# First diffusion step: VectorE checks a pair first and then copies the mixed sums of its first tile

## The reference

```python
def _top_p_attention(X, W1, W2, W3):
    q = X @ W1.T @ W2.T
    k = X @ W3.T
    probs = jax.nn.softmax(q @ k.T / TAU, axis=-1)
    idx = jnp.argsort(-probs, axis=-1)
    sp = jnp.take_along_axis(probs, idx, axis=-1)
    cs = jnp.cumsum(sp, axis=-1)
    keep_sorted = cs - sp < TOP_P          # TOP_P = 0.9
    ...
    A = probs * mask
    return A / jnp.maximum(A.sum(-1, keepdims=True), 1e-12)
R = S + jnp.eye(N); R = R / R.sum(-1, keepdims=True)
for n in range(STEPS):                     # STEPS = 2
    A = _top_p_attention(Xa, W1, W2, W3)
    Xf = R @ Xf
    Xa = A @ Xa
    Z = Z + Xf @ U1[n].T + Xa @ U2[n].T
```

## Time and profile before

| | |
|---|---|
| median of three runs | 2990.27 us |
| the profiled execution's own time | 2988.41 us |
| its span, first to last instruction | 2986.7 us |
| mean granted TensorE clock | 0.895 of full speed |
| the first diffusion step, about | 900 to 1449 us of the span |

### The profile page before, as it was taken

One profiled execution on the slowest core, in us unless ns is written; L12 is line 12 of the kernel. 1 busy time (PEld: TensorE's weight loads), 2 busy tenths in 40 slices (PEclk: granted clock), 3 DMA queues, 4 the chain that ended last, 5 costly groups with the idle time before them and its releaser, 6 DMA issues. The chain is left out here.

```text
span 2986.7 us, 44231 instructions
## 1 busy us (share of the span) xinstructions
PE 2314.8 (78%) x14310; PEld 1703.0 (57%) x14310; DVE 1941.0 (65%) x4668; ACT 1224.8 (41%) x1981; POOL 662.2 (22%) x1649
## 2 busy tenths in 40 slices
PE   3499999589536999996844974877563599999999
PEld 2377777377315787775523763766462244444468
DVE  5567777523337877777238888888965577777741
ACT  3455566211346666661256863766422100000000
POOL 2000000200224444340025643555402200000000
PEclk9699999899768999998966987989787799999999
DMA  1322221054100000000100000000004000000013
GB/s 46 119 98 97 97 81 68 5 191 145 42 17 13 19 23 19 22 27 14 48 17 6 16 11 11 16 11 16 11 11 155 2 1 0 0 0 0 0 50 96
DMA packets 49299, 120.85 MB, mean 40 GB/s; under 512 B 5952, under 2 KB 24672, under 8 KB 45792
## 3 DMA queue, kind: packets, MB, share of 16 engines
q1 hardware_dynamic: 49120, 118.83, 11.8%
HBM read 93.85 MB, written 24.97 MB: 40 GB/s over the span
## 5 line engine op out<-in xcount | busy, mean ns | idle before, releaser
L1923 DVE SCALAR_TENSOR_TENSOR fil_acc<-bank,fil_node,fil_acc 128x256 f32<-128x256 f32 x682 | 330.0, 484 | 110.4 <-PE bank L1991 97.8
L1346 PE MATMUL bank<-idf,X 128*128 128x128 f32 x968 | 136.2, 302 | 202.9 <-DVE step_recips L1841 202.9
L1436 ACT ACTIVATE step_PT<-bank 128x512 f32<-128x512 f32 (+1 forms) x264 | 127.5, 577 | 357.4 <-PE bank L1346 357.4
L1989 PE MATMUL bank<-parts_in,fil_xTh 128*128 128x512 f16 x704 | 268.5, 381 | 0.0
L1991 PE MATMUL bank<-parts_in,fil_xTl 128*128 128x512 f16 x704 | 268.3, 381 | 0.0
L1990 PE MATMUL bank<-parts_in,fil_xTh 128*128 128x512 f16 x704 | 268.2, 381 | 0.0
L1346 PEld LDWEIGHTS bank<-idf,X 128*128 128x128 f32 x968 | 119.4, 154 | 215.4 <-DVE step_recips L1841 206.2
L722 PE MATMUL bank<-V,HL 128*128 128x256 f32 x968 | 236.4, 386 | 0.2
L1356 PE MATMUL bank<-kH,qHL 128*128 128x512 f16 (+1 forms) x264 | 105.9, 401 | 151.9 <-ACT step_E L1445 117.7
L1378 PE MATMUL bank<-A,step_PT 128*128 128x256 f32 x968 | 216.1, 379 | 0.0
L1378 PE MATMUL bank<-H,step_PT 128*128 128x256 f32 x968 | 216.0, 379 | 0.0
(11 more groups left out here) (382 smaller groups left out, 5044.4 us busy)
## 6 DMA issues: line engine op xcount, KB each, us to landing
gat_A<-in_adj SPq DMA_DIRECT2D x22, 1408.0 KB, 5.9
step_a<-adjT SPq DMA_DIRECT2D x44, 352.0 KB, 3.0
gcn_raw<-in_L_W SPq DMA_DIRECT2D x16, 512.0 KB, 4.7
split<-gcn_halves SPq DMA_DIRECT2D x16, 512.0 KB, 3.4
parts_in<-split SPq DMA_DIRECT2D x4, 2048.0 KB, 19.2
adjT<-gat_a SPq DMA_DIRECT2D x22, 352.0 KB, 2.3
gcn_a<-adjT SPq DMA_DIRECT2D x22, 352.0 KB, 3.9
out_a<-adjT SPq DMA_DIRECT2D x22, 352.0 KB, 2.9
```

Source lines behind the costliest of these rows:

```text
L1346: last = pe.transpose(p_bank[n % nb][:, i * 128:i * 128 + 128], M[j][:, (b + i) * 128:(b + i) * 128 + 128], core.idf[:])
L1436: act.activation(PT[:, b * 128:(b + m) * 128], p_bank[n % len(p_bank)][:, 0:m * 128], ACT.Copy).then_inc(pT_done, 1)
L1923: c(dve.scalar_tensor_tensor(out=acc[k][:], in0=ps, scalar=node[k][:, n:n + 1], in1=acc[k][:], op0=ALU.mult, op1=ALU.add))
L1989: pe.matmul(w_bank[n % 4][:], xTh[k][:, x], wh[:, blk], start=c == 0, stop=False)
```

## The change

In VectorE's list for a step with one estimate, `check` and `finish_0` change places. Nothing is added or removed.

```diff
             if evals == 1:
                 in_order(dve, [take_1, below_0, largest_0, below_1, finish_1,
-                                take_0, sort, keep_0, largest_1, keep_1, finish_0, check], T // 2)
+                                take_0, sort, keep_0, largest_1, keep_1, check, finish_0], T // 2)
```

## The result

The changed kernel takes 2986.87 us (median of 20 runs, 2984.45 to 2990.74), the kernel before 2992.1 us (20 runs, 2988.0 to 2997.43). The ratio is 0.9978, with a 95% interval of 0.9972 to 0.9985: 0.22% faster, some 6.6 us, where 8.9 were forecast (the two medians themselves lie 5.2 us apart; the changed kernel's was forecast at 2981.4, in a range of 2976.5 to 2990.5). The profiled execution of the kernel before (2988.41 us) is one of its fastest, so the two spans, 2986.7 and 2985.9 us, say less than the ratio. The second profile of the changed kernel has a span of 2979.9 us. In the first profile of the changed kernel, 2.9 us were lost before the diffusion step begins, 1.6 in its first pair, and 3.1 behind the step; in none of the three stretches was an instruction moved.

The account below looks back on a forecast made before the run. TensorE was taken as nearly full, 43.48 us of an ordinary pair's 45.44. Ordinary pairs 3.0, loop entry 5.8, jump back 2.3, repeated search -2.2 sum to 8.9 us: median 2981.4 us, 8-in-10 range 2976.5 to 2990.5.

Parts of the forecast that it names:

- the ordinary pairs: First diffusion step, ordinary pairs of tiles at 45.4 us: 0.6 us less each, counted for five of six, 3.0 us.
- the jump back: Where VectorE's loop jumps back, 51.54 us from copy to copy: 2.3 us less, the 6.39 us stall staying.
- The copy's wait goes: Copy L1575 waits 42.6 us for `mix`; the change moves this stall, but at most 1.96 us per ordinary pair can be won.
- The floor of a pair: Time to which an ordinary pair can fall: taken as 44.8 us, from 45.4.
- a bound from ScalarE of 44.5: Ordinary pair: ScalarE's 22.25 us from one exponential to the next, its 0.86 us wait excluded, taken twice.
- The new ring through L1368: Each pair: check, F and copy, then TensorE from `neighbours` to the end of `attend`: 44.0 us, under ScalarE's 44.5.
- The entry: Pair entering the loop, 49.64 us: 5.8 us less, 2.4 from TensorE's shorter gap, 3.4 from keeping the full clock.
- The repeated search: Pair whose check repeats its search: 2.2 us lost, because TensorE's `neighbours` must now wait for the copy behind it.
- The slower rival: A second stall of some 2.9 us ahead of the copy in each pair delays `neighbours`: 3006 us, chance 0.08.

Follow-up runs that it names:

- new order in the loop only: Changed order only in the four rounds of the hardware loop (6 to 9), old order elsewhere, against the kernel before: 2987.09 us, ratio 0.9979.
- written out: Old order, VectorE's rounds of the first step all written out with no loop on VectorE, against the kernel before: 2986.78 us, ratio 0.9976.
- the kernel with the old order there: Changed kernel, but in round 10, whose check repeats its search, the copy stands ahead of the check: 2981.33 us, ratio 0.9958 to the kernel before.

## Why the prediction was right, and where its terms were off

The sign, the sum (8.9 us forecast, 8.4 in the step, 6.6 by the ratio) and the mechanism held. That the sum came so near is in part luck: the ordinary pairs gave 2.4 us more than forecast and the jump back 2.0 less. By its steps:

- **The copy's wait goes, and TensorE limits what that is worth.** Right. L1557's wait took most of it over (27.0 to 50.7 us), as said. The floor of a pair was put at 44.8 us by adding some tenths to a bound from ScalarE of 44.5; it is 44.2, with TensorE 98.6% busy. The 44.5 was no bound. It counted the time from one exponential to the next as ScalarE's own, less one wait; but ScalarE is busy for only 31.04 us of a pair, and in the half round that was doubled it waits 3.10 us for GpSimd (at 1289.98) and 1.36 for TensorE (at 1299.63). The ordinary pairs in the table gave 5.4 us and not 3.0, 1.1 each instead of 0.6. The first, which the forecast left out, gave 1.4 us. Of the terms that came out larger than forecast, this was off the most.
- **The new ring through L1368, 44.0 us, stays just under the rest.** Right, and close: in two pairs inside the loop L1368 did wait 0.3 us for the copy. One more instruction of 2.98 us ahead of the copy makes it the bound at once (3027.18 us).
- **The entry.** Right in size (5.4 of 5.8: the gap 2.6 for 2.4, the clock 2.8 for 3.4) and in the clock, which fell there in the three profiles with the old order in the rounds ahead and both searches in the program (before, new order in the loop only, written out), and in none of those with the new order and no extra maximum ahead of the copy. The name was wrong: the stall before L1557 is not made by the loop. And a part of the gain was luck: VectorE came earlier also because that stall no longer showed, on which the prediction did not count. The Trainium skill, page "TensorE: Matmul & The Clock Gate" (Part 1), says that the throttled clock is the default and that activity releases it. The traces at the entry agree: gaps of 2.95 to 3.37 us were followed by a fall, and those of 0.21 and 2.10 us were not.
- **The jump back.** Wrong by 2.0 us. VectorE did bring the 2 us, and the clock took 1.7 of them: the stretch at 1.2 GHz had been hidden under a wait and was so no longer. The prediction named TensorE's long gap at the jump back and even a shorter cold stretch there as a gain; it did not ask where the stretch would land.
- **The repeated search.** Right in kind. It costs 2.7 us in the profile and 3.0 against the kernel with the old order there, where 2.2 were said; the matmuls now start at the low clock (6.26 us for 44, against 4.97).
- **The slower rival.** It did not come: the stall behind the check's jumps stayed inside the check, and F followed the reciprocals at once (idle for at most 0.36 us). The price was understated: 15.7 us were said for a stall of 2.9 us ahead of the copy, and with a maximum of 2.98 us there the kernel is 33.5 us over the one before.

What stays open: what decides in which rounds VectorE has a second stall of 2 to 3.6 us before L1557, with and without a loop. And the time behind the step differs by about 3 us between the two profiles of the changed kernel (1541.3 and 1538.4 us), with equal code; the cause is not shown. Single spans of this kernel can't be compared closer than that.

## What to carry to other kernels

A wait on an engine that is not the bound is worth only what the engines behind it lose by it: look for the last one that waits, and at how full it is. Before an instruction is put behind a longer one, add up the ring that closes through whoever waits for its result, here an estimate of 44.0 us in a pair of 45.4, and look at the one case where the longer one takes very long. A rare slow path can be given its own order where the code is written out.

## What the runs showed of the hardware

- What a stretch at TensorE's lower clock costs here depended on where it landed. At the jump back the 14 matmuls took 3.19 us in one kernel and 3.03 in the other, for 1.69 at the full clock; in the one it cost nothing, since TensorE waited another 1.79 us behind it, in the other 1.7 us. This is read from the traces; no run isolates it.
- Skipping code costs time on VectorE: with the two conditional blocks and the jumps over them out of the program the idle time in the check fell from 3.1 to 1.5 us each, and the 6.4 us at the jump back went. The Trainium skill, page "Runtime: NRT & Kernel Launch" ("Instruction fetch mechanics"), says that a jump to code that is not at hand has to fetch it first. These two numbers agree with it; they do not separate the blocks' length from the jumps themselves.
- The one jump back of VectorE's loop costs 6.6 us of the step (51.53 against 44.95 us with VectorE's rounds written out) as long as the two blocks are in the loop's body; without them that pair takes 44.6 us with the loop (old order).
